# Attention of layer 0: two heads in 32 rows of weighted values, row sums by products with ones, output product by batches

## The chip, the cores and the metric

The kernel runs on one core of a Trainium2 chip. All data is float32 (the mask is a byte per element). The metric is the device time of one execution in microseconds.

## What is computed

A two-layer block over x of 8 batches x 256 rows x 256 columns, with a context of the same shape. Layer 0 is a cross attention of 16 heads of width 16, then a feed-forward network with FP4 rounding in blocks of 16. Layer 1 is a masked cross attention of 16 heads of width 64, then a feed-forward network with a piecewise linear GELU. The part that the change touches is the attention of layer 0:

```python
Qh, Kh, Vh = heads(layernorm(x) @ Wq.T + bq), heads(ctx @ Wk.T + bk), heads(ctx @ Wv.T + bv)
scores = einsum('bhqd,bhkd->bhqk', Qh, Kh) / 4
attn = softmax(scores - max)               # over the 256 keys
attn = clip(attn, 1e-12, None)
attn = attn / sum(attn)                    # a second division
ctx = einsum('bhqk,bhkd->bhqd', attn, Vh)
x = x + ctx.reshape(b, s, 256) @ Wo.T + bo
```

Then come a layer norm of x and the FP4 rounding of its result, which the gate and up products of the network read.

## The kernel before, in words

The 2048 rows are worked in 4 groups of 512 rows: 2 batches, 4 tiles of 128 rows. Each engine has one hand-written list of work. TensorE (PE) writes to 8 PSUM banks of 128x512; a planner (`Jobs`, `Pass`) gives each product its bank, and counting semaphores per bank (`filled`, `drained`) order the engines. There is no other scheduling: an engine does its list in order, and a wait holds up all behind it.

One group passes these stages: attention 0 (`layer0_heads`), the norm and rounding (`quantized_norm`), then `fp4_and_layer1` (FP4 network, attention 1 and its output product). Behind it stand the inputs of layer 0 of the next group and the last network of this group (`last_hidden`, `gelu`, `last_out`). So `layer0_heads` runs once in the opening (group 0, from 31 us to 107 us, with the rounding and transposing of the FP4 weights among it) and three times in a "crossing" between groups (from 293, 538 and 785 us on).

Attention 0 has 32 units (head x batch), `unit0`, worked in 8 rounds of 4. In iteration r of its loop PE issues, in this order: the weighted values of round r-2 (`layer0_weighted`, L1095), a key chunk of layer 1 for round r-1 (`layer1_key`, L991 through `product`), the transposes of the probabilities of two units of round r-1 (L1006), the scores of round r (`layer0_scores`, L1074), the transposes of the other two units. ScalarE (ACT) copies each transposed unit out of PSUM (L488), the key chunk (L537), every second round the weighted values (`weighted`, L551, into `c0raw`), and takes the exponentials of round r (L544). VectorE (DVE) takes row maxima (L796) and inverts sums, scales and clips (L801, L804); in rounds 2 to 5 of a crossing it also finishes an output tile of the group before (L779, L781).

Each head stands in 32 rows of the weighted values: 16 of values, one of ones (column 16 of `v0`, set at L403), which gives the sum of the clipped probabilities, and 15 of zeros. So 4 heads fill 128 rows and 16 heads 4 "quads". A product with a matrix `spread_s` copies each sum to the rows of its head (`spread_sums`, L1107), DVE multiplies the quad by 2 minus the sum (L827), and `layer0_out` (L1115) multiplies the four quads, zero rows included, with `wo0_s`, whose row 16 holds the bias bo. Tile by tile (`residual_and_ln_tile`, L738, L709) DVE adds x and takes statistics; GpSimd (POOL) makes the reciprocal root (L410); DVE normalises (L723) and rounds in two halves of two tiles (`quantize`, L666 to L691); PE transposes a half (L999) and begins the gate and up products. Between `layer0_out` and these transposes PE does three value products of layer 1 (`VALUES_FIRST`).

## Time and profile before

| what | value |
|---|---|
| time, median of 3 runs | 1039.73 us (1037.31 to 1040.15) |
| the profiled execution's own time | 1037.55 us |
| its span in the trace | 1035.7 us, so 1.85 us lie around it |
| PE busy | 916.5 us, 88% |
| VectorE busy | 737.4 us, 71% |
| ScalarE busy | 584.7 us, 56% |
| GpSimd busy | 187.1 us, 18% |
| chain of work that ended last | PE 55%, DVE 29%, ACT 8% |
| mean granted TensorE clock | 0.988 |

PE is busy for most of the span, yet no engine bounds the whole: the chain goes from engine to engine. Which one ends last is read stretch by stretch. In the views of the trace, PE shows each float32 product as two matmul instructions, so "x16" at L1095 is 8 products.

### The profile page before, as it was taken

The numbers are of one execution on the slowest core, as the hardware profiler recorded it, in microseconds if no ns is written. First come the engines' busy times: TensorE is split into PE (matmuls) and PEld (weight loads), VectorE is DVE, ScalarE is ACT, GpSimd is POOL, SyncE is SP. The second block draws the span as 40 slices with busy tenths as digits, with TensorE's granted clock in tenths as the row PEclk, the third lists the DMA queues.
The fourth block names the chain that finished last, engine by engine and source line by source line (L and its number), as shares of the span: only waits on it lengthen the run. The fifth ranks groups of instructions, "written<-read, shape, count | busy, mean of one in ns | idle before, by whom it ended". The sixth has DMA issues, their size and how long they took to land.

```text
span 1035.7 us, 15288 instructions
## 1 busy us (share of the span) xinstructions
PE 916.5 (88%) x5092; PEld 588.1 (57%) x5092; DVE 737.4 (71%) x2290; ACT 584.7 (56%) x1641; POOL 187.1 (18%) x301
## 2 busy tenths in 40 slices
PE   3778999999979999899978989999997898989985
PEld 1444664667555556466655556466755555646743
DVE  6799893673889697374598879367388969737358
ACT  1578322882679532695468922388267953269442
POOL 2000000672000000375000000067200000037400
PEclk8999999999999999999999999999999999999989
DMA  9400000000000000000000000000000000000000
GB/s 290 169 1 2 26 0 21 2 1 1 1 1 16 6 26 0 22 2 1 1 1 11 12 26 1 20 1 2 1 1 1 20 3 1 0 1 2 1 1 20
DMA packets 15308, 18.47 MB, mean 18 GB/s; under 512 B 3585, under 2 KB 12417, under 8 KB 15233
## 3 DMA queue, kind: packets, MB, share of 16 engines
q1 hardware_dynamic: 13168, 15.80, 4.8%
q10 hardware_dynamic: 2064, 1.71, 0.6%
q8 instruction: 42, 0.69, 0.3%
q14 instruction: 34, 0.27, 0.1%
HBM read 15.41 MB, written 2.10 MB: 17 GB/s over the span
## 4 chain that ended last, share of the span: by engine, by line
PE 55%; DVE 29%; ACT 8%; issue 4%; SPq 2%; DMA 1%; POOL 0%; POOLq 0%; DVEq 0%
PE bank L991 24%; PE bank L1006 8%; PE bank L1191 5%; PE bank L1272 5%; PE bank L1169 4%; ACT ring L488 3%; PE bank L1074 3%; PE bank L1095 3%; DVE row_max L796 2%; ACT ring L579 2%; PE bank L1115 2%; DVE block_max L666 1%; DVE ring L687 1%; DVE ring L689 1%; DMA w_s<-w 1%
## 5 line engine op out<-in xcount | busy, mean ns | idle before, releaser
L410 POOL TENSOR_TENSOR rstd<-var_eps,minus_half 128x2 f32<-128x2 f32 x32 | 24.2, 760 | 683.6 <-DVE var_eps L718 683.6
L488 ACT ACTIVATE ring<-bank 128x512 f32<-128x512 f32 x228 | 124.3, 591 | 28.4 <-PE bank L1006 28.1
L421 POOL TENSOR_TENSOR ring<-ring,row_inv 128x256 f32<-128x256 f32 x192 | 112.2, 615 | 98.5 <-DVE row_inv L888 98.5
L1006 PEld LDWEIGHTS bank<-ident_s,ring 128*128 128x128 f32 x768 | 85.1, 142 | 53.8 <-issue 28.7
L1006 PE MATMUL bank<-ident_s,ring 128*128 128x128 f32 x768 | 105.5, 279 | 10.9 <-DVE ring L804 7.3
L579 ACT ACTIVATE ring<-ring,row_max 128x256 f32<-128x256 f32 x192 | 95.4, 500 | 14.2 <-DVE row_max L881 13.8
L544 ACT ACTIVATE ring<-bank,row_max 128x256 f32<-128x256 f32 x192 | 88.3, 491 | 21.7 <-DVE row_max L796 21.7
L991 PE MATMUL bank<-ctxT_s,wk_s 128*128 128x512 f32 x160 | 81.1, 631 | 17.2 <-DVE wk_s L953 7.1
L796 DVE TENSOR_REDUCE row_max<-bank 128x2 f32<-128x512 f32 x128 | 79.4, 682 | 15.6 <-PE bank L1074 15.6
L881 DVE CUSTOM_DVE_ANT_0 ring<-bank,maskbias 128x256 f32<-128x256 f32 x192 | 69.9, 420 | 19.3 <-issue 19.3
L991 PE MATMUL bank<-wgu_s,act_s 128*128 128x352 f32 x256 | 80.5, 468 | 2.8 <-ACT act_s L482 2.8
L1041 PE MATMUL bank<-w_s,big_q 128*128 128x256 f32 x256 | 61.8, 388 | 19.0 <-DVE big_q L768 18.9
L991 PE MATMUL bank<-wv_s,ctxT_s 128*128 128x512 f32 (+1 forms) x192 | 73.5, 522 | 0.0
L574 ACT ACTIVATE big_v<-bank 128x512 f32<-128x512 f32 x32 | 19.1, 597 | 95.8 <-PE bank L991 95.8
L1191 PE MATMUL bank<-ring,big_v 128*64 128x256 f32 x512 | 69.2, 392 | 0.0
L1169 PE MATMUL bank<-big_q,big_k 64*128 64x256 f32 x512 | 63.9, 389 | 4.9 <-ACT big_k L616 4.9
L1041 PEld LDWEIGHTS bank<-w_s,big_q 128*128 128x128 f32 x256 | 46.8, 190 | 34.9 <-DVE big_q L768 26.7
L991 PEld LDWEIGHTS bank<-wgu_s,act_s 128*128 128x128 f32 x256 | 48.3, 193 | 28.3 <-ACT act_s L482 3.7
L991 PE MATMUL bank<-act_s,w_s 128*128 128x512 f32 x128 | 59.0, 621 | 3.4 <-ACT act_s L482 2.7
L804 DVE TENSOR_SCALAR ring<-ring,row_inv 128x256 f32<-128x256 f32 x192 | 59.1, 350 | 3.4
L1169 PEld LDWEIGHTS bank<-big_q,big_k 64*128 64x128 f32 x512 | 47.5, 186 | 24.1 <-issue 20.4
L991 PE MATMUL bank<-act_s,wq_s 128*128 128x512 f32 x128 | 57.0, 598 | 3.1 <-issue 3.1
(155 smaller groups left out, 1697.5 us busy)
## 6 DMA issues: line engine op xcount, KB each, us to landing
ctxT_s<-ctxT SPq DMA_DIRECT2D x4, 512.0 KB, 3.7
x_s<-x SPq DMA_DIRECT2D x4, 512.0 KB, 4.0
w_s<-w SPq DMA_DIRECT2D x2, 1024.0 KB, 15.7
out<-act_s SPq DMA_DIRECT2D x16, 128.0 KB, 1.7
wk_s<-wk SPq DMA_DIRECT2D x1, 1024.0 KB, 11.4
wv_s<-wv SPq DMA_DIRECT2D x1, 1024.0 KB, 13.5
wq_s<-wq SPq DMA_DIRECT2D x1, 1024.0 KB, 15.6
wo_s<-wo SPq DMA_DIRECT2D x1, 1024.0 KB, 17.8
```

Source lines behind the costliest of these rows:

```text
L421: ins = pool.tensor_tensor(probs1[i % PRING1][:, a, :], probs1[i % PRING1][:, a, :], row_inv[:, i, a:a + 1].to_broadcast([P, SEQ]), ALU.mult)
L488: act.activation(probsT[u % TRING][:, :, :].rearrange("p a q -> p (a q)"), psum(at, key)[:], ACT.Copy).then_inc(drain(at, key), 1)
L544: ins = act.activation(probs0[i % PRING0][:, a, :], psum(at, ("s0", i))[:, a * SEQ:(a + 1) * SEQ], ACT.Exp, bias=row_max[:, i, a:a + 1], a ...
L579: ins = act.activation(probs1[i % PRING1][:, a, :], probs1[i % PRING1][:, a, :], ACT.Exp, scale=-1.0, bias=row_max[:, i, a:a + 1], accum_o ...
L796: dve.tensor_reduce(row_max[:, i, :], psum(at, ("s0", i))[:].rearrange("p (a k) -> p a k", a=2), AX_X, ALU.max, negate=True).then_inc(max0, 1)
L804: ins = dve.tensor_scalar(probs0[u % PRING0][:, a, :], probs0[u % PRING0][:, a, :], row_inv[:, u, a:a + 1], CLIP, ALU.mult, ALU.max)
L881: ins = dve.tensor_tensor_reduce(probs1[i % PRING1][:, a, :], psum(at, ("s1", i))[:, a * SEQ:(a + 1) * SEQ], maskbias[:, 2 * b + a, :], -1 ...
L991: ins = pe.matmul(dst, lhsT, rhs, start=(n == 0), stop=(n == len(pairs) - 1))
L1006: ins = pe.transpose(psum(at, key)[:, c * SEQ + a * P:c * SEQ + (a + 1) * P], tile[:, a, c * P:(c + 1) * P], ident_s[:])
L1041: ins = pe.matmul(psum(at, key)[:, 0:DM], yT[:, m, t * P:(t + 1) * P], w2_s[:, m, :], start=(m == 0), stop=(m == FC1 - 1))
L1169: ins = pe.matmul(psum(at, key)[:, a * SEQ:(a + 1) * SEQ], q1[rows, p, b * SEQ + a * P:b * SEQ + (a + 1) * P], k1[rows, p, b * SEQ:(b + 1) ...
L1191: ins = pe.matmul(psum(at, key)[DK1 * j:DK1 * (j + 1), b * SEQ:(b + 1) * SEQ], v1[:, 2 * b + c, DK1 * head:DK1 * (head + 1)], probsT[u % T ...
```

## The change

- `unit0` takes the batch ahead of the quad: rounds 0 and 1 are quads 0 and 1 of the first batch, rounds 2 and 3 the same quads of the second, rounds 4 to 7 the other two quads. An even round holds the even heads, an odd round the odd heads.
- `v0` holds for two heads [even values, 16 zero columns, odd values]. The even head's product takes columns 0 to 31 of it, the odd head's columns 16 to 47, and both accumulate in the same 32 rows. The weighted values of two rounds so lie in half a bank, with no zero rows left.
- The sums come from products of the same transposed probabilities with a matrix of ones (`ones_by_head`) in the other half of the bank: 8 more products a round. The `spread` products and `spread_s` go.
- ACT no longer copies the weighted values; it makes 2 minus the sum (`inverse_sum`, 128x256) every second round. DVE multiplies (`over_sums`, 128x256) in rounds 3, 5 and 7, and for the last time within `quantized_norm`.
- The output product has 2 chunks of 128 full rows for 4 quads: 8 products for 16, by batches of two tiles. The first batch's four come right behind the first transposes of the last round; the second batch's four come at the end, in a crossing behind one of the three value products. DVE adds x and takes statistics by halves (`sum_half`).
- The bias bo is added to x by GpSimd (`bias_x`, 128x1024) in a step of its own; DVE waits for it (`x_biased`).
- In PE's and ACT's lists the key chunk of layer 1 stands ahead of the weighted values and of the transposed copies.
- `wo0` is loaded by 2 DMAs of its true rows in place of 8 with zero rows; `spread` is replaced by a broadcast of bo.

```diff
 def unit0(i):
-    return i // 8, i // 4 % 2, i % 4
+    return 2 * (i // 16) + i // 4 % 2, i // 8 % 2, i % 4
...
+        def head_columns(pair):
+            flat = pair.rearrange("p n d -> p (n d)")
+            return flat[:, 0:PAD0], flat[:, DK0:DK0 + PAD0]
...
-            for j in range(4):
-                for n in range(2):
-                    src = wo0.rearrange("(c j n r) d -> j n r c d", c=2, j=4, n=2)[j, n]
-                    dst = wo0_s[PAD0 * j:PAD0 * (j + 1), :, :].rearrange("p (c n) d -> p c n d", n=2)[:, :, n, :]
-                    sp.dma_start(dst, src).then_inc(rest_loaded, 16)
+            for c in range(HEAD_CHUNKS):
+                rows = wo0.rearrange("(c h r) d -> c h r d", c=HEAD_CHUNKS, r=PAD0)[c, :, 0:DK0, :]
+                sp.dma_start(wo0_s[:, c, :], rows).then_inc(rest_loaded, 16)
...
+            def bias_x(g):
+                pool.wait_ge(xn_ready, (0 if g == 0 else 4 * g - 1) * TILES + TILES)
+                pool.tensor_tensor(x_s[:], x_s[:], bo0_s[:].unsqueeze(1).to_broadcast([P, TILES, DM]), ALU.add).then_inc(x_biased, 1)
...
                 ln_power(g * 4 + 4)
+                bias_x(g + 1)
...
-                def weighted(quad):
-                    key = ("pv0", quad)
-                    act.wait_ge(*is_filled(at, key))
-                    act.activation(c0raw[:, quad, :], psum(at, key)[:], ACT.Copy).then_inc(drain(at, key), 1)
+                def inverse_sum(w):
+                    act.wait_ge(*is_filled(at, ("pv0", w)))
+                    act.activation(over_sum, psum(at, ("pv0", w))[:, SEQ:2 * SEQ], ACT.Identity, bias=two[:], scale=-1.0).then_inc(over_sum_ready, 1)
...
                     if r >= 1:
                         first = 4 * (r - 1)
+                        layer1_key(at, r - 1)
                         for i in (first, first + 1):
                             evacuate_probsT(at, 0, i)
-                        layer1_key(at, r - 1)
...
+            def over_sums(at, w, group):
+                c, b, key = w // 2, w % 2, ("pv0", w)
+                dve.wait_ge(over_sum_ready, group * WEIGHTED0 + w + 1)
+                dve.tensor_tensor(c0[:, c, b * SEQ:(b + 1) * SEQ], psum(at, key)[:, 0:SEQ], over_sum, ALU.mult).then_inc(drain(at, key), 1)
...
                     for i in round_units0(r):
                         row_maxima(i)
+                    if r >= 3 and r % 2 == 1:
+                        over_sums(at, (r - 3) // 2, units // UNITS)
...
-                for t in range(2):
-                    residual_and_ln_tile(at, "o0", t, x_s, res_a, n)
-                ln_variance(n, 0)
-                residual_and_ln_tile(at, "o0", 2, x_s, res_a, n)
+                dve.wait_ge(x_biased, g + 1)
+                sum_half(0)
                 ln_normalize(n, 0, res_a, xn)
-                quantize_half(0, last_tile)
+                over_sums(at, WEIGHTED0 - 1, g)
+                quantize_half(0, lambda: sum_half(1))
...
+                for summed in range(2):
+                    for c in range(2):
+                        for u in round_units0(r):
+                            j = unit0(u)[2]
+                            pair = ones_by_head[:] if summed else v0[:, 2 * b + c, head0(quad, j) // 2, :, :]
+                            ins = pe.matmul(psum(at, key)[PAD0 * j:PAD0 * (j + 1), summed * SEQ:(summed + 1) * SEQ], head_columns(pair)[odd],
+                                            probsT[u % TRING][:, c, :], start=(odd == 0 and summed == 0 and c == 0), stop=(odd == 1 and summed == 1 and c == 1))
...
+            def layer0_out(at, h):
+                key = ("o0", h)
+                pe.wait_ge(*is_drained(at, ("pv0", WEIGHTED0 - HALVES + h)))
+                wait_free(at, key)
+                for n in range(2):
+                    t = 2 * h + n
+                    for c in range(HEAD_CHUNKS):
+                        ins = pe.matmul(psum(at, key)[:, n * DM:(n + 1) * DM], c0[:, c, t * P:(t + 1) * P], wo0_s[:, c, :],
+                                        start=(c == 0), stop=(c == HEAD_CHUNKS - 1))
+                ins.then_inc(fill(at, key), 1)
...
                 for r in range(1, ROUNDS0 + 2):
+                    if r <= ROUNDS0:
+                        layer1_key(at, r - 1)
                     if r >= 2:
                         layer0_weighted(at, r - 2)
                     if r <= ROUNDS0:
-                        layer1_key(at, r - 1)
                         first = 4 * (r - 1)
                         layer0_transposes(at, group, (first, first + 1))
                         if r < ROUNDS0:
                             layer0_scores(at, r)
                         else:
-                            spread_sums(at, [0])
+                            layer0_out(at, 0)
                         layer0_transposes(at, group, (first + 2, first + 3))
...
-                        if r == ROUNDS0:
-                            spread_sums(at, range(1, QUADS - 1))
-                spread_sums(at, [QUADS - 1])
-                layer0_out(at)
+                if not with_weights:
+                    values(middle_pass(group), *VALUES_FIRST[0])
+                layer0_out(at, 1)
```

## Rows read from the trace of the kernel before

**Rows 1.** The page: shares of the chain that ended last, by engine.
```profile
PE 55%; DVE 29%; ACT 8%; issue 4%; SPq 2%; DMA 1%; POOL 0%; POOLq 0%; DVEq 0%
```

**Rows 2.** Timeline, PE, one crossing round: start, duration, line, operation, count, idle before.
```profile
337.55 1.07 PE L1095 MATMUL bank<-ring,v 128*32 128x256 f32 x16 [0.83 <-ACT ring L488]
338.56 1.98 PE L991 MATMUL bank<-ctxT_s,wk_s 128*128 128x512 f32 x4
340.38 1.04 PE L1006 MATMUL bank<-ident_s,ring 128*128 128x128 f32 x8
341.34 1.15 PE L1074 MATMUL bank<-big_k 32*128 32x256 f32 x16
342.42 1.09 PE L1006 MATMUL bank<-ident_s,ring 128*128 128x128 f32 x8
344.34 1.02 PE L1095 MATMUL bank<-ring,v 128*32 128x256 f32 x13 [0.83 <-ACT ring L488]
```

**Rows 3.** Windows, one round: length, then busy PE, PEld, DVE, ACT, POOL; clock, DMA.
```profile
331.84:338.62 6.78, 5.95 (x53) 3.68 (x53) 6.17 (x19) 6.26 (x23) 0.00 (x0) 1.00 0.07 22
```

**Rows 4.** Timeline, DVE, the row maxima of that round.
```profile
342.51 2.48 DVE L796 TENSOR_REDUCE row_max<-bank 128x2 f32<-128x512 f32 x4 [0.60 <-PE bank L1074]
```

**Rows 5.** The page, groups: line, operation, count, busy us, mean ns of one, idle before.
```profile
L421 POOL TENSOR_TENSOR ring<-ring,row_inv 128x256 f32<-128x256 f32 x192 | 112.2, 615 | 98.5 <-DVE row_inv L888 98.5
```

**Rows 6.** The chain in order of time: scores of layer 1, two side by side.
```profile
193.47 1.93 PE bank L1169 x16
```

**Rows 7.** Timeline, PE, from the last round to the gate and up products.
```profile
347.16 1.04 PE L1006 MATMUL bank<-ident_s,ring 128*128 128x128 f32 x8
...
348.90 1.04 PE L1006 MATMUL bank<-ident_s,big_k 128*128 128x128 f32 x8
349.77 1.88 PE L991 MATMUL bank<-big_c,spread_s 128*128 128x512 f32 x4
351.58 1.07 PE L1095 MATMUL bank<-ring,v 128*32 128x256 f32 x16
...
354.33 7.07 PE L1115 MATMUL bank<-wo_s,big_c 128*128 128x256 f32 x32
361.24 5.31 PE L991 MATMUL bank<-wv_s,ctxT_s 128*128 128x512 f32 x12
367.77 0.66 PE L999 MATMUL bank<-ident_s,act_s 128*128 128x128 f32 x4 [1.22 <-DVE act_s L691]
...
369.11 5.00 PE L991 MATMUL bank<-wgu_s,act_s 128*128 128x352 f32 x16 [0.69 <-ACT act_s L482]
```

**Rows 8.** Timeline, DVE, the same stretch.
```profile
357.56 0.42 DVE L738 TENSOR_TENSOR res_a<-bank,x_s 128x256 f32<-128x256 f32 x1 [2.33 <-PE bank L1115]
...
360.52 0.74 DVE L723 TENSOR_SCALAR act_s<-res_a,moments,rstd 128x256 f32<-128x256 f32 x2
...
363.93 0.68 DVE L676 TENSOR_TENSOR ring<-act_s,inv_scale 128x512 f32<-128x512 f32 x1
```

**Rows 9.** Timeline, the end of attention 0 in the opening, DVE and PE.
```profile
106.81 1.88 DVE L827 SCALAR_TENSOR_TENSOR big_c<-bank,big_c 128x512 f32<-128x512 f32 x3
...
122.66 0.60 PE L999 MATMUL bank<-ident_s,act_s 128*128 128x128 f32 x4
```

**Rows 10.** The page: what the DMA engines moved in each fortieth of the span.
```profile
GB/s 290 169 1 2 26 0 21 2 1 1 1 1 16 6 26 0 22 2 1 1 1 11 12 26 1 20 1 2 1 1 1 20 3 1 0 1 2 1 1 20
```

**Rows 11.** Timeline, PE: gate and up products of group 2, transposes of the last group.
```profile
614.09 6.69 PE L991 MATMUL bank<-wgu_s,act_s 128*128 128x352 f32 x16 [0.69 <-ACT act_s L482]
...
989.15 0.66 PE L999 MATMUL bank<-ident_s,act_s 128*128 128x128 f32 x4 [2.57 <-DVE act_s L723]
```

**Rows 12.** Windows (columns as in rows 3), the stretch around those transposes.
```profile
988.00:998.00 10.00, 8.12 (x15) 3.57 (x16) 2.28 (x5) 1.96 (x3) 0.33 (x1) 0.66 0.01 2
```

**Rows 13.** Timeline, DVE: beside GpSimd's mask work, and the last norm before a crossing.
```profile
19.30 1.75 DVE L691 TENSOR_TENSOR act_s<-big_v,scale 128x768 f32<-128x768 f32 x1
...
254.48 0.73 DVE L723 TENSOR_SCALAR act_s<-act_s,moments,rstd 128x256 f32<-128x256 f32 x2 [0.81 <-POOL rstd L410]
```

More of the change, by code:

```diff
@@ L42 @@
 ROUNDS0 = UNITS // 4
+WEIGHTED0 = ROUNDS0 // 2
+HEAD_CHUNKS = HEADS * DK0 // P
 GELUS = 5
@@ L102, in jobs_layer0 @@
         jobs.add(("t0", i), 4 + i % 2)
-    for q in range(QUADS):
-        jobs.add(("pv0", q), 6)
+    for w in range(WEIGHTED0):
+        jobs.add(("pv0", w), 6)
     for r in range(1, ROUNDS0 + 1):
@@ L108, in jobs_layer0 @@
             jobs.add(("w", r - WEIGHTS_FROM), 7)
-    for q in range(QUADS):
-        jobs.add(("sum0", q), q)
-    for t in range(TILES):
-        jobs.add(("o0", t), 4 + t)
+    for h in range(HALVES):
+        jobs.add(("o0", h), h)
     return jobs
@@ L138, in jobs_middle @@
     jobs = Jobs()
-    for key, place in zip(VALUES_FIRST, (0, 1, 6)):
+    for key, place in zip(VALUES_FIRST, (2, 3, 6)):
         jobs.add(("v1",) + key, place)
@@ L427, in _ @@
             mask_to_bias()
+            pool.wait_ge(rest_loaded, 16 * 5)
+            bias_x(0)
             for g in range(GROUPS - 1):
@@ L460, in _ @@
             act.dma_start(bv0_s[:], bv0.partition_broadcast(P)).then_inc(values_loaded, 16)
-            act.dma_start(spread_s[:], spread).then_inc(rest_loaded, 16)
+            act.dma_start(bo0_s[:], wo0[DK0, :].partition_broadcast(P)).then_inc(rest_loaded, 16)
             act.dma_start(b1_s[:], b1).then_inc(rest_loaded, 16)
@@ L567, in layer0_heads @@
                             exponentials(i)
-                weighted(QUADS - 1)
+                inverse_sum(WEIGHTED0 - 1)
             def evacuate_values(at, t, n):
@@ L1086, in layer0_weighted @@
                 quad, b, _ = unit0(4 * r)
-                key = ("pv0", quad)
-                if b == 0:
+                key, odd = ("pv0", r // 2), r % 2
+                if not odd:
                     wait_free(at, key)
@@ L1091, in layer0_weighted @@
                     pe.wait_ge(*is_drained(at, ("t0", u)))
-                for c in range(2):
-                    for u in round_units0(r):
-                        j = unit0(u)[2]
-                        ins = pe.matmul(psum(at, key)[PAD0 * j:PAD0 * (j + 1), b * SEQ:(b + 1) * SEQ], v0[:, 2 * b + c, head0(quad, j), :],
-                                        probsT[u % TRING][:, c, :], start=(c == 0), stop=(c == 1))
-                if b == 1:
+                for summed in range(2):
[5 more added lines that the diff above has]
+                                            probsT[u % TRING][:, c, :], start=(odd == 0 and summed == 0 and c == 0), stop=(odd == 1 and summed == 1 and c == 1))
+                if odd:
                     ins.then_inc(fill(at, key), 1)
@@ L1199, in fp4_and_layer1 @@
                 per_group = 10 * QUANTS
-                for t, n in VALUES_FIRST:
+                for t, n in VALUES_FIRST[1 if g > 0 else 0:]:
                     values(at, t, n)
```

74 lines of the change are left out of this document (28 added, 46 removed).

## Prediction

> **What bounds the kernel now.** The page's chain [rows 1] names no single engine: PE 55%, DVE 29%. So I took its pieces in order of time, went to the four runs of attention 0 and their ends, which are all that the diff touches, and read there the timelines of PE, DVE and ACT side by side.
>
> In a crossing the eight rounds repeat every 6.79 us: L1095 starts at 337.55 and 344.34 [rows 2]. The reader is to see the 0.83 us of idle PE before each L1095: the last transposes start at 342.42, ACT must copy both units out, and only then do the weighted values start, 1.92 us later. That loop of PE and ACT is the bound. DVE (6.17 of 6.78) and ACT (6.26) are nearly full too [rows 3].
>
> Behind the rounds the bound changes hands. From the last weighted values (351.58) the chain runs through a copy, a spread product, a DVE product and part of the output products to the first add at 357.56, then through DVE alone until the first half is rounded and transposed at 367.77 [rows 7, 8]. PE has 16 output products and three value products meanwhile, and still idles 1.22 us. From the transposes at 367.77 on PE is bound by little but itself, so what this moment gains the group keeps.
>
> In the opening DVE sets the rounds (it rounds weights too), and the transposes at 122.66 stand right behind PE's value products [rows 9].
>
> **The rounds.** From start to start the PE steps of a round are 1.01 (weighted), 1.82 (key chunk), 0.96 (transposes), 1.08 (scores) and then 1.92 (transposes and the wait) [rows 2]. Now the key chunk follows those transposes and covers ACT's copies: transposes alone take 0.87 (348.90 to 349.77 [rows 7]), so the idle 0.83 goes and about 1.05 of the 1.92 with it. The weighted values double. They are 128x32 products, four side by side. One product of 256 columns takes 0.43 us (354.33 to 361.24, 6.91 us for 16 [rows 7]), and eight in groups of four take 1.07 [rows 2], twice 0.43 and a start of 0.2. Eight more are two more groups, +0.86, so the step is 1.87. The new round is 1.82 + 1.87 + 0.96 + 1.08 + 0.87 = 6.60 us, 0.19 less. Seven such steps save 1.3 us.
>
> **The new wait.** The even round's weighted values start a bank that DVE must have emptied (`over_sums`), and that multiply is queued behind four row maxima. From the scores' start it is 1.17 to the maxima, 2.4 for the four, 0.42 for the multiply (an add of that size takes 0.42 [rows 8]) and a handover: 4.05 [rows 2, 4]. PE comes there after 1.08 + 0.87 + 1.82 = 3.77. It waits 0.3, with DVE late by its finished tiles 0.4, three times a run: +1.0, with the transposes, the scores and so ACT's exponentials queued behind it. Bounds: 0 and 0.8 a time. ACT's short product has half the columns of the copy that it replaces, so ACT's 6.3 us [rows 3] become at most 6.6 in an odd round and still fit. Rounds in all: -0.3 us in a crossing.
>
> **The end of a crossing.** Let X be the start of the last round's first transposes; before, X = 347.16 and the half's transposes came at X + 20.6 [rows 7]. After:
> - four output products of the first batch, 0.43 each, filled at X + 2.8; the other transposes start at X + 2.6; the weighted values 1.92 later at X + 4.5; with 16 products they end at X + 6.5.
> - DVE: add, statistics, root on GpSimd and normalise took 357.56 to 361.26, 3.7 us [rows 8]; now from X + 2.8 to X + 6.4, beside PE and ACT.
> - ACT's 2 minus sum 0.4, multiply 0.45: X + 7.3. DVE is held at it for 0.5 to 0.9 us, and the rounding queued behind it.
> - block maxima and scales: between 361.26 and 363.93 lay 2.67 us, of which the last tile's add and statistics took about 1.2; 1.5 are left: X + 8.9.
> - PE: one value product 1.72 (X + 8.2), second batch 1.74, filled at X + 10.1. DVE's add and statistics of half 1 about 2.0: X + 12.1.
> - the rest of the rounding took 363.93 to 367.77, 3.8 us [rows 8, 7]: transposes at X + 15.9.
>
> That is 4.7 us earlier, with the rounds 5.0; three crossings give 15 us. PE's two other value products end at X + 13.4, so they are hidden; PE then idles 2.5 us. Half 1 of the rounding stands as far behind half 0 as before.
>
> **The opening.** DVE sets its rounds, so three multiplies of 0.36 to 0.42 are paid: +1.1. The key chunk ahead of the weighted values now waits for ACT's copy of transposed weights (same bank); PE waits for DVE in each of those rounds; I take 0, with a bound of 1.5, about two of the 0.86 steps above. The last rounding of weights ends at 106.81 [rows 9], now 107.9. The first batch's output product is long done; add to normalise 3.6, multiply 0.4: 111.9. PE: output products 1.7, weight transposes 1.3, three value products 5.2: 120.2, against 122.66 [rows 9]: -2.5. PE begins these rounds only when the last layer 1 weights have landed, while the DMA engines move 290 GB/s [rows 10]. The transfers before that shrink by 256 KB of `wo0` and grow by 64 KB of a broadcast: -0.6 (bounds -1.5 and 0). Opening: -3.1.
>
> **Other edits.** `bias_x` is 128x1024 on GpSimd, estimated at 2.5 us from 0.615 us for 128x256 [rows 5]; it is needed 90 us later. It starts beside DVE's last norm (254.48 [rows 13]). Beside GpSimd's mask work a DVE product took 1.75 us [rows 13] for the usual 0.96, 0.8 more; PE needs that norm about 1.5 us after its end. I take 0 (bounds 0 and 1 us a crossing).
>
> The Trainium skill, "SBUF — State Buffer", section "Who interferes with whom", says that a GpSimd operation that reads SBUF and a Vector one with two SBUF inputs or in a two-port mode lock each other out for a whole instruction. The trace agrees that they slow each other, though by 0.8 us, not by the whole of the mask work.
>
> **The clock.** Gate and up products of group 2 took 6.69 us [rows 11] for 5.00 [rows 7], 1.7 us more with the same idle before it, because the clock had fallen; it happened in one crossing of three. In the last group PE idles 2.57 us, does four transposes, idles again [rows 11], and the granted clock of that stretch is 0.66 [rows 12], so partly at 1.2 GHz for 2.4. The new 2.5 us of idle looks like this one, where the old was 1.22. I take one fall more than before, +1.7 us; bounds none and three more, -1.7 and +6.
>
> **Sum.** -15.0 - 3.1 + 1.7 = -16.4 us on the profiled execution's 1037.55: 1021.2. The median of the runs lies 2.2 above that execution, so I forecast 1023 us.
>
> **Rivals.**
> 1. *The clock falls at every transition*, four or five at 1.7 us: 1028. For: the gap of 2.57 us and the clock behind it [rows 11, 12]. Against: that is one case, and PE had been as busy before the old gaps, of which one in three cost the clock. Chance 0.14.
> 2. *GpSimd's add holds the last norm back* for its whole 2.5 us; PE's slack of 1.5 is gone, 1 us three times: 1026. The skill's rule above would do this. Chance 0.10.
> 3. *The products with ones cost more than two groups.* If they go two side by side (as L1169's eight take 1.93 [rows 6]) they add 1.72 a round, PE's round is 7.46, the new wait vanishes under it. A crossing pays 8 x 0.86 - 1.0 = 5.9 more, 17.6 in all, and the opening, whose PE loop then passes DVE's, some 4: 1045, slower. It decides from about 0.7 us more a round. Against: the products of L1095 have the same shape and go in fours. Chance 0.07.
> 4. *The early half brings nothing*, because DVE is held in the multiply or PE by the second batch longer than worked out; only the shorter chain is gained, 1.5 us a crossing: 1035, or no change that can be told. Chance 0.06.
>
> Forecast 0.63.
>
> **How the numbers follow.** The forecast's own bounds are 1018 (no new wait, no clock fall) and 1029; rival 1 and 2 lie within. Up to 1034 about one case in ten is left out, below 1016 hardly any. Range 1016 to 1034. A measurement tells 0.3%, 3.1 us: rival 3 with a tail of the others is slower, 0.07; rival 4 splits: same 0.05; faster 0.88.
>
> **What would show it.** L1095 as x32 at about 1.9 us, with a round of 6.6 to 7.0 and no wait for L488; every second L1095 released by DVE's multiply after 0.3 to 0.4; the first add of `sum_half` within 3 us of the last round's first transposes; transposes of the half 16 us behind them for 20.6; a granted clock of 1.00 or not after the idle before them. A round above 7.3, or a first add that waits on PE at the end, makes the prediction wrong.

## The result, and the profile after

| | before | after |
|---|---|---|
| median of 4 runs each, same chip | 1039.16 us | 1028.29 us (1026.96 to 1029.1) |
| ratio, 95% interval | | 0.9896 [0.9878, 0.9914] |
| the profiled execution's own time | 1037.55 us | 1028.21 us |
| its span | 1035.7 us | 1026.3 us |
| mean granted TensorE clock | 0.988 | 0.981 |
| PE, VectorE, ScalarE, GpSimd busy | 916.5, 737.4, 584.7, 187.1 us | 919.7, 738.4, 583.0, 196.3 us |

The change is 1.0% faster. Forecast was 1023 in 1016 to 1034: sign and range held, but in the profiled executions 9.3 us went where 16.4 were worked out. The chain of the page after, to be laid beside [rows 1]:

```profile
PE 50%; DVE 33%; ACT 8%; issue 4%; SPq 2%; DMA 1%; POOL 1%; POOLq 0%; DVEq 0%
```

PE lost five points of the chain and DVE took four of them. To find where 7 us are missing, both traces were cut at the same instructions of PE: the first gate product of each group, the first product of layer 1's network behind the last norm (`act_s,w_s`), the first scores of each crossing and the end.

| stretch of PE's timeline | before | after | moved | forecast |
|---|---|---|---|---|
| start to the gate of group 0 | 124.00 | 125.00 | +1.0 | -3.1 |
| each crossing's first scores to the next gate, three times | 76.36 | 73.38 | -3.0 | -5.0 |
| gate to the network of layer 1, groups 0, 1, 3 | 134.35, 134.21, 129.79 | 134.55, 134.55, 129.88 | +0.6 in all | 0 |
| the same, group 2 | 135.89 | 134.55 | -1.3 | fewer or more falls of the clock: +1.7 for the whole run |
| network to the next scores, three times | 34.40 | 34.41 | 0 | 0 |
| the last stage | 45.16 | 44.37 | -0.8 | 0 |

They add up to the 9.4 us between the spans. So the crossings brought 9 us for 15, and the opening lost 1 for a gain of 3.

*A round in a crossing.* Timeline, PE, two rounds of after (start, duration, line, operation, count, idle before):

```profile
320.97 1.07 PE L1118 MATMUL bank<-ring,v 128*32 128x256 f32 x16 [0.20 <-DVE big_c L807]
321.86 1.05 PE L1118 MATMUL bank<-ring,ones_by_head 128*32 128x256 f32 x16
322.84 1.09 PE L1027 MATMUL bank<-ident_s,ring 128*128 128x128 f32 x8
323.86 1.15 PE L1095 MATMUL bank<-big_k 32*128 32x256 f32 x16
324.94 1.09 PE L1027 MATMUL bank<-ident_s,big_k 128*128 128x128 f32 x8
325.87 1.88 PE L1012 MATMUL bank<-ctxT_s,wk_s 128*128 128x512 f32 x4
327.68 1.07 PE L1118 MATMUL bank<-ring,v 128*32 128x256 f32 x16
...
334.66 1.07 PE L1118 MATMUL bank<-ring,v 128*32 128x256 f32 x16 [0.20 <-DVE big_c L807]
```

The idle 0.83 behind ScalarE's copies [rows 2] is gone from these rounds. From 320.97 the weighted values and the products with ones take 1.87 us together. The rounds take 6.71 and 6.97 in turn (320.97, 327.68, 334.66), 6.84 on average against 6.79 before; every second one waits for DVE's multiply (`big_c L807`).

*The end of the crossing.* Timeline, PE, then DVE, of after:

```profile
350.15 1.09 PE L1027 MATMUL bank<-ident_s,ring 128*128 128x128 f32 x8
351.08 1.89 PE L1134 MATMUL bank<-wo_s,big_c 128*128 128x256 f32 x8
...
358.36 1.89 PE L1134 MATMUL bank<-wo_s,big_c 128*128 128x256 f32 x8
360.09 3.60 PE L1012 MATMUL bank<-wv_s,ctxT_s 128*128 128x512 f32 x8
366.01 0.66 PE L1020 MATMUL bank<-ident_s,act_s 128*128 128x128 f32 x4 [2.32 <-DVE act_s L705]
367.35 5.00 PE L1012 MATMUL bank<-wgu_s,act_s 128*128 128x352 f32 x16 [0.69 <-ACT act_s L495]
```

```profile
353.08 0.69 DVE L857 TENSOR_TENSOR res_a<-bank,x_s 128x512 f32<-128x512 f32 x1 [1.47 <-PE bank L1134]
...
357.18 0.42 DVE L807 TENSOR_TENSOR big_c<-bank,big_c 128x256 f32<-128x256 f32 x1 [0.57 <-ACT big_c L564]
...
360.29 0.69 DVE L857 TENSOR_TENSOR res_a<-bank,x_s 128x512 f32<-128x512 f32 x1 [1.28 <-PE bank L1134]
```

The last round's first transposes start at 350.15, the first add comes 2.93 later (353.08), the half's transposes 15.86 later (366.01). Before they came 20.6 later [rows 7]. The whole gain of a crossing is in this stretch.

*The start of the crossing.* PE waits there for DVE, which empties four tiles of the last network's output. PE after, then the windows that begin with that key chunk, after and before (length, busy PE, PEld, DVE, ACT, POOL, granted clock, DMA):

```profile
299.09 2.55 PE L1012 MATMUL bank<-ctxT_s,wk_s 128*128 128x512 f32 x4 [2.05 <-DVE act_s L788]
301.44 1.91 PE L1027 MATMUL bank<-ident_s,ring 128*128 128x128 f32 x8
303.28 1.34 PE L1095 MATMUL bank<-big_k 32*128 32x256 f32 x16
304.55 1.09 PE L1027 MATMUL bank<-ident_s,ring 128*128 128x128 f32 x8
```

```profile
299.10:304.60 5.50, 5.50 (x29) 3.33 (x29) 2.63 (x11) 2.31 (x6) 0.00 (x0) 0.69 0.00 0
```

```profile
297.87:303.50 5.63, 4.92 (x36) 3.16 (x36) 4.35 (x14) 3.21 (x9) 0.00 (x0) 1.00 0.00 0
```

The key chunk took 2.55 us where before the same one took 1.96, and the transposes behind it 1.91 for about 1.04. The granted clock is 0.69 and was 1.00: part of the stretch ran at 1.2 GHz for 2.4. All three crossings of after show it, none of before. A stretch at the lower clock is called a fall here.

*The opening.* PE after, the last rounds and the end of attention 0, where before the transposes came at 122.66 [rows 9]:

```profile
99.15 1.98 PE L1012 MATMUL bank<-ctxT_s,wk_s 128*128 128x512 f32 x4 [0.98 <-ACT wgu_s L489]
101.61 1.07 PE L1118 MATMUL bank<-ring,v 128*32 128x256 f32 x16 [0.47 <-DVE big_c L807]
...
112.06 3.31 PE L1134 MATMUL bank<-wo_s,big_c 128*128 128x256 f32 x8 [2.13 <-DVE big_c L807]
115.17 2.09 PE L1037 MATMUL bank<-ident_s,big_v 128*128 128x128 f32 x12
118.41 5.42 PE L1012 MATMUL bank<-wv_s,ctxT_s 128*128 128x512 f32 x12 [1.15 <-ACT wd_s L489]
123.66 0.60 PE L1020 MATMUL bank<-ident_s,act_s 128*128 128x128 f32 x4
```

Three things stand here that the sum had at nothing: a key chunk that waits 0.98 for ScalarE's weight copy; output products and weight transposes of 3.31 and 2.09 (the clock); and 1.15 of waiting ahead of the value products, whose first bank ScalarE has still to empty of transposed weights (`wd_s L489`).

*The last norm before a crossing*, DVE after, against 0.73 before [rows 13]; then GpSimd's bias add beside it:

```profile
255.35 2.76 DVE L737 TENSOR_SCALAR act_s<-act_s,moments,rstd 128x256 f32<-128x256 f32 x2 [0.81 <-POOL rstd L415]
```

```profile
255.28 2.36 POOL L433 TENSOR_TENSOR x_s<-x_s,bo_s 128x1024 f32<-128x1024 f32 x1
```

DVE's line holds two instructions. The first lasts from 255.35 to 257.78, 0.14 us past the end of GpSimd's (257.64); the second takes its usual 0.4.

### The profile page after: what moved, and what is told of

Read it like the earlier page. It is cut to its first block, busy times and chain, and to the rows that moved or that the text cites. A ratio compares the mean times of both kernels' runs of the same rounds, so it can differ in the third digit from the quotient of the medians.

```text
span 1026.3 us, 16101 instructions
## 1 busy us (share of the span) xinstructions
PE 919.7 (90%) x5508; PEld 586.6 (57%) x5508; DVE 738.4 (72%) x2282; ACT 583.0 (57%) x1641; POOL 196.3 (19%) x307
## 4 chain that ended last, share of the span: by engine, by line
PE 50%; DVE 33%; ACT 8%; issue 4%; SPq 2%; DMA 1%; POOL 1%; POOLq 0%; DVEq 0%
PE bank L1012 19%; PE bank L1027 8%; PE bank L1198 5%; PE bank L1279 5%; DVE row_max L815 4%; PE bank L1176 4%; PE bank L1118 3%; ACT ring L557 2%; PE bank L1095 2%; ACT ring L592 2%; ACT ring L501 2%; DVE ring L823 1%; PE bank L1134 1%; SPq L388 1%; DVE block_max L680 1%
## 5 line engine op out<-in xcount | busy, mean ns | idle before, releaser
L1027 PE MATMUL bank<-ident_s,ring 128*128 128x128 f32 x768 | 108.3, 285 | 5.3 <-ACT ring L501 2.6
## 6 DMA issues: line engine op xcount, KB each, us to landing
wq_s<-wq SPq DMA_DIRECT2D x1, 1024.0 KB, 15.9
```

The lines of the kernel that those rows point to most:

```text
L1027: ins = pe.transpose(psum(at, key)[:, c * SEQ + a * P:c * SEQ + (a + 1) * P], tile[:, a, c * P:(c + 1) * P], ident_s[:])
```

## Experiments

The theory at this point: the rounds and the end are as worked out; what is missing is the clock (three falls at the crossings' starts, one in the opening), the bank in the opening, and little from GpSimd. The rival to it: the doubled products or the new order of the key chunk cost something in every round that was taken for hidden. Line numbers in the diffs are left out; "sc to gate" is the stretch from a crossing's first scores to the next gate product, 73.38 in after.

**1. Does the moment of the crossing decide the clock? Both kernels, moved.** A wait in SyncE's list, ahead of the first loads, moves the loads of the opening against the rest.

```diff
+            sp.wait_ge(consts_set, 7)      # after;  4 in the kernel before
             load_ctx(0)
```

> The changed kernel, with its first loads issued about 1.6 us later (SyncE first waits for GpSimd's constants), so that all later work shifts by about 1.6 us and nothing else changes. Theory A: the falls of the granted clock at the start of each crossing (5.5 us at 0.69, three times, 1.6 us lost each) depend on when the work happens to lie, not on its gaps, which are the same as before. Then at least some of the three falls go or move to other gaps; the time is 1.6 us later plus or minus what moves: between 1024 and 1032. Theory B: the doubled products or the new order cause the falls; then the three stay at the same places and the time is 1028.3 + 1.6 = 1029.9 with a clock of 0.69 behind each crossing's first key chunk.

> The kernel before, with its first loads issued about 2 us later, nothing else changed. Theory A (where the falls lie depends on when the work lies): the one fall in group 2 (1.7 us) goes or others appear, so that the time is not simply 2 us more: 1037 to 1045. Theory B (the fall belongs to the work): one fall, in group 2, and 1039.2 + 2 = 1041.2.

Measured: after moved 1026.92 us (1023.98 to 1029.7), ratio 0.9901 [0.9877, 0.9925], against after's 0.9896: no difference that can be told. Its loads landed no later (the first key chunk of attention 0 starts at 38.56, against 39.10). The falls of the clock in the opening at 38 and 113 us are gone and it reaches the gate at 120.92, 4.1 us earlier; one at 57 came. Timeline, PE, of this kernel at the end of the opening:

```profile
109.33 1.99 PE L1135 MATMUL bank<-wo_s,big_c 128*128 128x256 f32 x8 [2.13 <-DVE big_c L808]
...
114.33 5.42 PE L1013 MATMUL bank<-wv_s,ctxT_s 128*128 128x512 f32 x12 [1.12 <-ACT wd_s L490]
```

The same idle time of 2.13 stands ahead of the output product, and no fall follows. The three crossings, all 4.1 us earlier, kept their fall. Before moved: 1039.38, 1.002 [0.9995, 1.0044], gate at 125.78 for 124.00, and still no fall at a crossing's start. So 4 us of opening are worth nothing to the median of the runs that can be told from its spread, and this shift did not tell whether the place in time or the kernel makes the fall. Experiment 8 tells more.

**2. The new order of the key chunk, undone.** PE's key chunk and ScalarE's copy of it go back behind the weighted values and the first transposed copies.

```diff
                 for r in range(1, ROUNDS0 + 2):
-                    if r <= ROUNDS0:
-                        layer1_key(at, r - 1)
                     if r >= 2:
                         layer0_weighted(at, r - 2)
                     if r <= ROUNDS0:
+                        layer1_key(at, r - 1)
```

> The changed kernel with the key chunk of layer 1 again behind the weighted values on TensorE and behind the first two transposed copies on ScalarE. Theory 1 (the loop of TensorE and ScalarE bounds the rounds and the key chunk hides ScalarE's copies): a crossing's round becomes 1.87 + 1.82 + 1.02 + 1.08 + 1.92 = 7.7 us for 6.84, +0.87 seven times in three crossings, +18 us, about 1047. Theory 2 (ScalarE or VectorE already bounds the rounds): under +6 us.

Measured: 1060.52 us, ratio 1.0225 [1.0204, 1.0246], 32 us slower than after and slower than before. Timeline, PE, of this kernel:

```profile
823.26 1.07 PE L1118 MATMUL bank<-ring,v 128*32 128x256 f32 x16 [0.83 <-ACT ring L501]
831.94 1.07 PE L1118 MATMUL bank<-ring,v 128*32 128x256 f32 x16 [1.86 <-DVE big_c L807]
839.59 1.07 PE L1118 MATMUL bank<-ring,v 128*32 128x256 f32 x16 [0.83 <-ACT ring L501]
```

The old idle 0.83 is back in each round (7.65 us), and every second round pays 1.86 for the multiply (8.68), where after pays 0.20. The expectation had only the 0.83. The key chunk covers two waits: ScalarE's copies and DVE's multiply. In the third crossing, which has no fall of the clock at its start, sc to gate is 80.70; the kernel of experiment 8 takes 71.7 there. The order is worth 9 us a crossing, 27 in all, more than the 11 us of the whole change.

**3. The new order alone, in the kernel before.**

```diff
+                    if r <= ROUNDS0:
+                        layer1_key(at, r - 1)
                     if r >= 2:
                         layer0_weighted(at, r - 2)
                     if r <= ROUNDS0:
-                        layer1_key(at, r - 1)
```

> The kernel before with one part of the change alone: the key chunk of layer 1 ahead of the weighted values on TensorE and ahead of the transposed copies on ScalarE. Theory 1 (the order hides ScalarE's copies, and it is this that pays for the doubled products): TensorE's loop shrinks from 6.79 to 5.8 us, so that ScalarE (6.3 and 6.8) or VectorE (6.2, 6.8 with a finished tile) binds at about 6.5; seven rounds in three crossings, -0.3 each, -6 us, about 1032.5; no change in the opening, where VectorE sets the pace. Theory 2 (the order gives nothing by itself): within 2 us of before.

Measured: 1038.84 us (1035.37 to 1041.18), ratio 1.0009 [0.9994, 1.0025]: no change, where 6 us less were expected. Timeline, PE, of this kernel:

```profile
553.98 1.42 PE L1006 MATMUL bank<-ident_s,ring 128*128 128x128 f32 x8
555.80 1.15 PE L1074 MATMUL bank<-big_k 32*128 32x256 f32 x16 [0.40 <-ACT big_k L544]
556.88 1.09 PE L1006 MATMUL bank<-ident_s,big_k 128*128 128x128 f32 x8
557.80 1.88 PE L991 MATMUL bank<-ctxT_s,wk_s 128*128 128x512 f32 x4
559.62 1.07 PE L1095 MATMUL bank<-ring,v 128*32 128x256 f32 x16
```

The round is 6.64 us (552.98 to 559.62) for 6.79. PE now waits for ScalarE's exponentials, 0.40 ahead of the scores: ScalarE, at 6.26 of 6.78 [rows 3], is the bound that lay right behind the old one. In the crossing without a fall sc to gate is 75.63, 0.7 less; in the other two, which start with a fall, 77.3: 1.7 more. The opening reached the gate at 124.99 instead of 124.00; most of that 1.0 us comes in its last round, where the key chunk waits 0.98 for ScalarE's weight copy. So the order by itself gives a round 0.15 us; what it does for the change is to make the doubled products free.

**4. The output product of the first batch, late.** `layer0_out(at, 0)` goes from behind the last round's first transposes to right ahead of the second batch's.

```diff
-                        else:
-                            layer0_out(at, 0)
...
+                layer0_out(at, 0)
                 layer0_out(at, 1)
```

> The changed kernel with the first batch's four output products moved from behind the last round's first transposes to right ahead of the second batch's. Theory 1 (the early half lets VectorE begin its norm beside the last weighted values): the first add comes about 5.5 us later for a last round 1.7 us shorter, the half's transposes at X + 19.9 for X + 15.9, +4 us in each of three crossings, +2 in the opening, about 1042. Theory 2 (the early half brings nothing, as rival 4 had it): within 3 us of 1028.

Measured: 1048.03 us, ratio 1.0103 [1.0082, 1.0124], 20 us slower than after for the 14 expected, and slower than before. Timeline, PE, the end of its second crossing:

```profile
607.06 1.89 PE L1134 MATMUL bank<-wo_s,big_c 128*128 128x256 f32 x8
612.96 3.78 PE L1134 MATMUL bank<-wo_s,big_c 128*128 128x256 f32 x8 [4.01 <-DVE big_c L807]
616.53 4.23 PE L1012 MATMUL bank<-wv_s,ctxT_s 128*128 128x512 f32 x8
622.49 0.66 PE L1020 MATMUL bank<-ident_s,act_s 128*128 128x128 f32 x4 [1.73 <-DVE act_s L705]
```

DVE does its adds and norm first and the last multiply after them, so PE waits 4.01 for it, and the clock falls in that idle time (3.78 us for products that take 1.89). The third crossing has no fall at its start and takes 77.32, 5.6 more than the crossings of experiment 8. A fall near its end, at 864 us, is in that figure: the output product at 862.20 takes 2.48 for 1.89, so up to 0.6 of the 5.6 is the clock. The late product costs about 5 us a crossing by place alone, close to the 4.7 of the prediction's tail. The early half is where the gain of the change sits.

**5. The multiply in the middle of the row maxima**, so that DVE reaches it 1.2 us earlier.

```diff
-                    if r >= 3 and r % 2 == 1:
-                        over_sums(at, (r - 3) // 2, units // UNITS)
+                        if i % 4 == 1 and r >= 3 and r % 2 == 1:
+                            over_sums(at, (r - 3) // 2, units // UNITS)
```

> The changed kernel with VectorE's multiply behind the second row maxima of its round, not behind the fourth. Theory 1 (the bank that the multiply empties holds up every even round of TensorE): the waits of 0.20 us in a crossing go, so that each pair of rounds takes 13.4 us for 13.68; three waits of about 0.25 in three crossings, -2.2 us; in the opening the waits of 0.76, 0.69 and 0.47 go too but VectorE sets the pace there, 0 to -0.5. Together about 1025.8 when the clock falls at the same places. Theory 2 (VectorE or ScalarE set the pace anyway): within 0.5 us of the changed kernel.

Measured: 1025.02 us (1023.63 to 1027.98), ratio 0.9864 [0.9841, 0.9886]. All rounds take 6.71 and none waits for DVE. Sc to gate is 72.67 with a fall at its start (73.38 in after), 71.00 without (71.7 in experiment 8): 0.7 less, as expected. The new wait costs 0.27 three times a crossing, and nothing is hidden behind it.

**6. Half of the products with ones.** They run over the first 128 keys only: the row sums lack half of the keys.

```diff
-                    for c in range(2):
+                    for c in range(1 if summed else 2):
```

> The changed kernel with the products with ones over the first 128 keys only (4 for 8 a round), so that the sums lack the other half of the keys. Theory 1 (TensorE's loop bounds a crossing's rounds, the products with ones are on it with 0.43 us for each group of four): the steps between first products of a round come down from 6.71 and 6.97 until ScalarE with 6.5 us of work binds, -0.25 seven times, and the last round is 0.43 shorter, -2.2 us a crossing, -6.5 in all, about 1022. Theory 2 (they are hidden): no change. In the opening VectorE sets the pace: no change by either.

Measured: 1023.22 us, ratio 0.9845 [0.981, 0.9881]. Timeline, PE, of this kernel:

```profile
319.49 1.07 PE L1118 MATMUL bank<-ring,v 128*32 128x256 f32 x16 [0.26 <-DVE big_c L807]
320.37 0.61 PE L1118 MATMUL bank<-ring,ones_by_head 128*32 128x256 f32 x8
320.92 1.09 PE L1027 MATMUL bank<-ident_s,ring 128*128 128x128 f32 x8
```

Four products less take 0.43 us less: they go four side by side, one group of four in the time of one. Of the seven times 0.43, 3.0 us, only 1.8 reach the end of the crossing (71.55 for 73.38 with a fall, 69.93 for 71.7 without). The rest turns into waits for the multiply (0.26) and for ScalarE's exponentials (0.30 ahead of scores). PE is the bound of after's rounds by less than half a microsecond.

**7. The bias add one norm later.** In a crossing GpSimd waits for DVE's last norm too, so that it adds while DVE has no norm to make.

```diff
-                pool.wait_ge(xn_ready, (0 if g == 0 else 4 * g - 1) * TILES + TILES)
+                pool.wait_ge(xn_ready, 4 * g * TILES + TILES)
```

> The changed kernel with GpSimd's add of the bias (crossings only) released by VectorE's last norm, not by the norm of the next group's input. Theory 1 (the add locks VectorE's norm out for its whole 2.4 us, seen as 2.76 us for 0.73): the norm takes 0.73 again and TensorE's wait of 0.27 before the last transposes goes, -0.3 us in each of three crossings, about -1.0. Theory 2 (VectorE's wait has another cause): the norm keeps its 2.7 us and the time stays.

Measured: 1025.81 us (1023.48 to 1026.86), ratio 0.9864 [0.9847, 0.9882]. Timeline, DVE:

```profile
251.41 0.74 DVE L737 TENSOR_SCALAR act_s<-act_s,moments,rstd 128x256 f32<-128x256 f32 x2 [0.80 <-POOL rstd L415]
```

The norm takes 0.74 again; the stretch from gate to network takes 134.29 and 134.20 for 134.55. The lock costs 2 us on DVE and 0.3 on the path. The larger difference of the medians is not the lock. In the profiles this kernel's opening reaches the gate at 121.00 for 125.00, again without the falls at 38 and 113 us; one crossing starts with a fall where after had three; and two falls came at the gates of groups 2 and 3 (gate to network 135.84 and 131.13).

**8. Other banks for the first value products**, so that the first isn't the bank of the last weight transposes.

```diff
-    for key, place in zip(VALUES_FIRST, (2, 3, 6)):
+    for key, place in zip(VALUES_FIRST, (3, 2, 6)):
```

> The changed kernel with the first value product in bank 3 and the second in bank 2, not the other way round. Theory 1 (in the opening the first value product waits 1.15 us for the last transposed weights to be copied out of bank 2): TensorE's wait goes and the gate of the opening comes 1.15 us earlier, -1.1 us; in the crossings no change. Theory 2 (VectorE sets that gate): no change.

Measured: 1024.55 us (1023.56 to 1025.71), ratio 0.9858 [0.9841, 0.9875]. Timeline, PE, of the opening's end, then of the first crossing's start with its window:

```profile
110.79 2.85 PE L1134 MATMUL bank<-wo_s,big_c 128*128 128x256 f32 x8 [2.12 <-DVE big_c L807]
113.43 2.44 PE L1037 MATMUL bank<-ident_s,big_v 128*128 128x128 f32 x12
115.70 5.32 PE L1012 MATMUL bank<-wv_s,ctxT_s 128*128 128x512 f32 x12
...
296.34 1.96 PE L1012 MATMUL bank<-ctxT_s,wk_s 128*128 128x512 f32 x4 [2.05 <-DVE act_s L788]
298.13 1.04 PE L1027 MATMUL bank<-ident_s,ring 128*128 128x128 f32 x8
```

```profile
296.30:301.90 5.60, 5.56 (x38) 3.65 (x39) 4.32 (x14) 3.17 (x10) 0.00 (x0) 1.00 0.00 0
```

The wait of 1.15 is gone. What was not expected: no crossing has a fall at its start. The gap ahead of the key chunk is the same 2.05 us and so is the work, but it lies 2.8 us earlier, and sc to gate is 71.73, 71.72 and 71.73, 1.66 less than after. This pair prices a fall at that place, since in a crossing the two kernels differ only by the exchanged banks. But the kernel isn't free of falls. Two came behind the idle time of 2.32 ahead of the half's transposes, at the gates of groups 2 and 3:

```profile
603.60 6.53 PE L1012 MATMUL bank<-wgu_s,act_s 128*128 128x352 f32 x16 [0.69 <-ACT act_s L495]
```

The gate to network stretches there take 136.05 and 131.47, 1.5 and 1.6 more than in after. So three falls went and two came at another gap: of the 5.0 us 3.1 were paid back.

**9. The three together, and an output tile in another order.** First experiments 5, 7 and 8 in one kernel; then with them

```diff
-                for t in range(TILES):
+                for t in (3, 0, 1, 2):
```

in `output_bias` of DVE's list: tile 3 lies in the bank that the first key chunk takes, and was emptied last.

> The changed kernel with the three mends together: the bias released by the last norm, the first value product in bank 3, the multiply behind the second row maxima. If each is worth what its own trace showed (0.3 us and 0.75 us in each crossing, 1.15 us once) the sum is -4.3 us, about 1023.5 against a before of 1038; clock falls may add or take 2 us.

> The three mends, and in round 0 of a crossing VectorE empties bank 7 (tile 3 of the last network's output) before the other three tiles. Theory 1 (the crossing's first key chunk waits 2.05 us for that bank): it starts 1.0 us earlier, the idle before it is 1.05 us, the first transposes follow 1 us earlier: -3 us in three crossings, and with a shorter gap the clock falls less often there; about 1020.5 against a before of 1038. Theory 2 (the first transposes wait for VectorE's clipping instead): they come at the same time and nothing is gained.

Measured: the three together 1025.31 us (1017.33 to 1028.41), 0.9863 [0.9831, 0.9896], no better than each alone: 1.8 us above the expectation. Its crossings take 72.70, 71.45 and 71.45 from scores to gate, the first with a fall, and its profiled execution has further falls at 113, 366, 605 and 847 us, with a mean clock of 0.976. Its runs lie 11 us apart. With the new order of the tiles 1020.92 us (1020.45 to 1021.36), 0.9834 [0.9819, 0.9848], as expected. Timeline, PE:

```profile
295.28 1.95 PE L1012 MATMUL bank<-ctxT_s,wk_s 128*128 128x512 f32 x4 [1.05 <-DVE act_s L788]
```

The gap ahead of the key chunk is 1.05 for 2.05, and sc to gate 70.37, 70.17 and 70.18, where the crossings of experiment 5 without a fall take 70.99: 0.8 from the gap itself. No crossing starts with a fall; two falls stand at the gates of groups 1 and 2 instead (gate to network 136.98 and 135.68).

**10. And one value product ahead of the second output product in the opening too.**

```diff
-                if not with_weights:
-                    values(middle_pass(group), *VALUES_FIRST[0])
+                values(middle_pass(group), *VALUES_FIRST[0])
```

> The kernel of the run before this one, and in the opening too the first value product stands ahead of the second batch's output product. Theory 1 (TensorE idles 2.1 us there for VectorE's multiply and sets the opening's gate): the product of 1.7 us fills the idle and the gate comes up to 1.7 us earlier, until VectorE's rounding binds, -1.5 us. Theory 2 (VectorE sets that gate already): no change.

Measured: 1016.06 us (1014.82 to 1019.62), ratio 0.9794 [0.9775, 0.9813]: the fastest of all, 2.1% below before and 11 us below after, each taken against the runs of before in its own session. Timeline, PE:

```profile
108.66 1.98 PE L1012 MATMUL bank<-wv_s,ctxT_s 128*128 128x512 f32 x4
111.52 1.99 PE L1134 MATMUL bank<-wo_s,big_c 128*128 128x256 f32 x8 [0.88 <-DVE big_c L807]
```

The value product fills the idle time ahead of the output product, 0.88 for 2.79 in the kernel without it, and the product behind it takes 1.99 for 3.47: no fall there. Against that the second value product, now the first behind the weight transposes, waits 1.12 for ScalarE's weight copy at 116.51: the bank wait of experiment 8 is back. The gate comes at 121.38 for 122.47, 1.1 us of the 1.5 expected, and how much of it is the missing fall these two profiles don't separate. The medians differ by 4.9, and the profiled spans only by 1.1 (1017.6 and 1018.7). The rest is the clock as far as the record tells: the three fastest runs of this kernel (1014.82 to 1016.06 us) have mean granted clocks of 0.987 and 0.988, its two others 0.982 and 0.983, and all four of the kernel without it 0.980 to 0.982.

## Why the prediction was right and where it was wrong

*The doubled weighted values: right.* 1.87 us for both, worked out as 1.87; the ones products add two groups of 0.43 (experiment 6). Rival 3 is out.

*The round: right in kind, off by 0.09.* 6.84 for 6.75. The two steps of transposes take 1.02 and 0.93 where 0.96 and 0.87 were carried over from before. Each now follows products of another tile size, and 0.06 came with it; the trace of before shows the same 0.06 (last section). The wait for the multiply costs 0.27 each time for 0.3 to 0.4 worked out. The step that carried most was that the key chunk covers the copies; experiment 2 shows that it covers more than that, and experiment 3 that ScalarE stands 0.04 us a round behind the 6.60 that were worked out.

*The end of the crossing: right to a tenth.* First add at X + 2.93 (X + 2.8), multiply held 0.57 (0.5 to 0.9), half's transposes at X + 15.86 (X + 15.9), idle before them 2.32 (2.5). Experiment 4 takes the early half away and the gain goes. Rival 4 is out.

*The clock: count and place were wrong.* The sum took one fall more, at the gate's idle time, for +1.7. There the trace of after shows none, and group 2's old one went too. Instead each crossing starts with a fall behind DVE's tile of output, an idle time of 2.05 us that both kernels have and that had cost nothing in any crossing before. 1.66 us each by experiment 8, 5.0 in all. With the falls in the opening it is the largest part of what is missing (sum below). That the doubled products by themselves put a fall at a crossing's start is excluded by experiment 8, which has them and no fall there. The failed step is that this gap was put at nothing without a reason, as if a gap which kept its clock three times of three would keep it. Over the twelve kernels with this gap of 2.05 us the fall followed in 3 of 3 crossings (after, after moved), in 2 of 3 (experiment 3), in 1 of 3 (experiments 2, 4, 5, 6, 7 and the first of 9) or in 0 of 3 (before, before moved, experiment 8): 14 of 36. The prediction's own gap, the idle time ahead of the half's transposes, was not wrongly suspected either: with 2.32 us of it the fall followed 14 times of 30 in the ten kernels that have it, none of them in after, and with the old 1.22 3 times of 9 (before, before moved, experiment 3). What sets it stays open.

Rival 1, falls at every transition for 1028 us, has the time that was measured, 1028.29, and its price of 1.7 a fall is right. Its place is not: in this kernel's profile no gate's idle time cost the clock. That its number came out is luck.

*The opening: wrong, by 4.1 us.* The second output product came at 112.06, worked out as 111.9, so the DVE side of the sum held: DVE's last row maxima start at 98.74 for 97.75 before, +1.0 of 1.1. Behind it the term "1.7 + 1.3 + 5.2", 8.3 us to the tenth, was mis-sized: it took 11.6. Part is the clock (window of 112 to 118.4 us: granted clock 0.73). Experiment 1's kernel, with the same idle time and no fall, takes 10.25 from the output product (109.33) to the half's transposes (119.58), so the fall is 1.35 of the 3.3. The other 2.0 are there without it: 1.12 to 1.15 is the wait for the bank, which experiment 8 removes, and most of the rest is the weight transposes, which take 2.04 for the 1.3 put down; before they took 1.47 and had no wait, now 0.35 goes into waiting for DVE's add to empty a bank. These waits were there to be found: the change gives each bank another order of owners, and only those in the crossings were followed.

The earlier landing of the weights was right (39.10 for 39.74), but that key chunk then took 3.75 us for 2.52 before, so nothing was left of it: the low clock at 38 us lasted longer than before's at 41. Without both falls, in experiments 1 and 7, the gate comes at 120.92 and 121.00, which is the forecast's -3.1. That sum came out by two misses that cancel, 2.0 us too little behind the output product and 2.0 too much ahead of it (109.33 for 111.3, the 111.9 less the landing's 0.6); the second is likely before's own fall at 41 us, taken over into the sum, which no run tests. The key chunk's wait of 0.98 for ScalarE's weight copy, taken at 0 with a bound of 1.5, is real; experiment 3 has it in the kernel before, with the opening 1.0 us longer.

*GpSimd's bias add: the mechanism of rival 2, at a third of its price.* DVE's norm took 2.76 us for 0.73: it makes no headway until GpSimd's 2.36 are over. The estimate of 0.8 came from another pair, DVE's 1.75 us at 19.30 [rows 13] beside GpSimd's mask work, which in the trace lasts from 19.20 to 21.98. That product stands within GpSimd's time from end to end and still took only 0.8 more, so one pair's price didn't carry to the other; why, no run shows. The Trainium skill, "SBUF — State Buffer", section "Who interferes with whom", says that such a pair locks each other out for a whole instruction, and for the bias add the trace agrees with it and not with my reading; for the pair at 19.30 it doesn't. By that rule the price was put at 1 us three times; the path shows PE idle for 0.27 (258.16, `act_s L737`), and experiment 7 gives back 0.3. The slack was larger than the 1.5 us assumed: PE still had transposes of another buffer to do.

*The sum of what is missing.* 16.4 forecast, 9.4 come between the spans, 7.0 short. Opening 4.1: its two falls, 1.35 and 2.7 by experiment 1's kernel; the bank's 1.15 is there but made up elsewhere. Crossings 6.05: 5.0 clock at their start, the rest the rounds, 0.36 a crossing. GpSimd's lock and what lies with it 0.6. Against that stand 3.0 between gate and network of group 2, where the fall of before [rows 11] went and the one added for the new idle time didn't come, and 0.8 in the last stage (granted clock in the 10 us from its network's start: 0.69 before, 0.78 after). Of the clock the sum had the price right, 1.7 a fall, and neither the count nor the places. All this is one profiled execution of each kernel. Over whole runs at the same mean granted clock, 0.981, eight of before average 1040.3 us and the four of after 1028.2: 12 us, where the stretches without falls add up to more. How much of the median's shortfall is the clock is so less sure than these sums.

## What to carry to other kernels

A gain that lies in moving work ahead (here: output products by halves) holds to a tenth of a microsecond when each engine's list is added up step by step, and the same sum shows which other step must cover the added work; undo that step alone before it is called a detail. Follow every buffer or bank whose order of owners changes in each stage that uses it, the opening included. And count the falls of the clock in the trace of before as a toss, not as a property of the gap: with the same gap and the same work they came and went with a shift of a few microseconds, 1.7 us each, so that single fixes of 1 us drown in them, and a fall that goes at one gap may come at the next. Filling the idle time is the fix to try first: with 2.05 cut to 1.05 the fall followed in 0 of 6 crossings, for 14 of 36 at 2.05. Six are few, and falls at the gates remained.

## What the runs showed of the hardware

- The granted clock behind an idle time of 2.05 us of PE, with the same work before and behind it: 1.00 at 297.87 in before and at 296.3 in experiment 8, 0.69 at 299.10 in after, and 0.70 at 298.80 in experiment 3's kernel. Price 1.66 us each. With 2.05 us the fall followed in 14 of 36 crossings, with 1.05 in 0 of 6.
- A GpSimd add of 128x1024 (2.36 us) beside DVE's 128x256 norms: 2.76 us for two that take 0.74 alone. The add of the opening, at 24.08, does the same to a DVE TENSOR_SCALAR of 128x768 (24.70): 2.58 us, where the next of that size takes 0.56. GpSimd's mask work cost a DVE product within its time only 0.8.
- Products of 128x32, four side by side: a group of four 256-column products takes 0.43 us, as long as one of 128x128 (with half of the products with ones 0.61 for 1.05).
- Transposes right behind products of another tile size take 0.06 us more to the next product than those behind 128x128 products (1.02 for 0.96, 0.93 for 0.87). The trace of before has both: 0.96 or 0.97 behind 128x128 products, 1.02 or 1.03 behind those of 64x128 and 128x64.
